# Feature sums of a graph network: four buffers for parts and masks, residues by pairs of visits, a square root's wait moved

## The reference

```python
x = x + _L0(h, edge_attr_16, src, dst, ...)   # 2 rounds: messages, segment_sum over dst, GRU
x = x + _L1(h, edge_index, ...)               # two GCN convolutions, dinv = rsqrt(degree + 1)
x = x + _L2(h, edge_index, edge_attr_16, ...) # mean of neighbours, last edge's features per node
x = x + _L3(h, edge_index, edge_attr_32, ...) # MLP on edges, segment_sum, GRU
```

## Time and profile before

| | us |
|---|---|
| median of 3 runs | 4950.62 (4948.92 to 4953.69) |
| the profiled execution | 4948.67 |
| its span, first to last instruction | 4946.6 |
| stretch of the feature sums, first mask's start to last mask's | 444 |
| from there to the build's first mask | 85 |

### The profile page before, as it was taken

One profiled execution on the slowest core, in us unless ns is written; L12 is line 12 of the kernel. 1 busy time (PEld: TensorE's weight loads), 2 busy tenths in 40 slices (PEclk: granted clock), 3 DMA queues, 4 the chain that ended last, 5 costly groups with the idle time before them and its releaser, 6 DMA issues. The chain is left out here.

```text
span 4946.6 us, 93310 instructions
## 1 busy us (share of the span) xinstructions
PE 3317.7 (67%) x24444; PEld 2513.4 (51%) x24445; DVE 2832.9 (57%) x7446; ACT 886.4 (18%) x1811; POOL 2097.5 (42%) x2644
## 2 busy tenths in 40 slices
PE   2333277777769889899989744555555666666666
PEld 1222123333329889798989633334444444444445
DVE  6555788777765544311323355555566666666775
ACT  1111113566650022200001100000000000000002
POOL 4666700000000021111111277777777777777770
PEclk6555699888889999999999755555555555555558
DMA  3000000111125424354544322223222333333330
GB/s 141 0 0 0 4 14 33 52 58 58 58 92 172 150 71 159 123 174 156 189 153 158 91 64 64 66 67 70 69 69 71 74 72 75 74 76 73 77 77 19
DMA packets 173539, 403.74 MB, mean 82 GB/s; under 512 B 47902, under 2 KB 109481, under 8 KB 172809
## 3 DMA queue, kind: packets, MB, share of 16 engines
q1 hardware_dynamic: 52409, 259.35, 14.7%
q10 hardware_dynamic: 69360, 91.59, 6.6%
q0 software_dynamic: 51680, 51.82, 6.0%
HBM read 359.52 MB, written 43.07 MB: 81 GB/s over the span
## 5 line engine op out<-in xcount | busy, mean ns | idle before, releaser
L697 POOL DMA_INDIRECT scr<-ptable,src_i x1566 | 1522.1, 972 | 481.6 <-issue 398.3
L666 POOL COPY late<-late 128x256 f32<-128x256 f32 (+1 forms) x65 | 25.8, 398 | 1949.6 <-POOLq L664 1949.6
L1030 PE MATMUL ps_front<-scr,arena 128*128 128x192 bf16 x7203 | 612.2, 248 | 67.2 <-PEq L1028 67.2
L1139 PE MATMUL ps_front<-stat_w,scr 128*128 128x392 fp8e4 x2064 | 494.2, 370 | 239.4 <-PEq L1143 214.3
L1030 PEld LDWEIGHTS ps_front<-scr,arena 128*128 128x128 fp8e4 x7203 | 601.0, 98 | 76.9 <-issue 74.9
L900 ACT ACTIVATE arena<-arena 128x384 f32<-128x384 f32 x309 | 161.6, 523 | 1859.9 <-ACTq L899 1859.9
L952 PE MATMUL ps_front<-arena 128*128 (+1 forms) x930 | 176.7, 363 | 434.3 <-PEq L950 434.3
L1651 DVE TENSOR_TENSOR scr<-scr,late 128x384 bf16<-128x384 f16 x1024 | 360.5, 352 | 183.7 <-DVEq L1650 176.4
L1139 PEld LDWEIGHTS ps_front<-stat_w,scr 128*128 128x128 bf16 x2064 | 187.8, 105 | 507.8 <-issue 467.0
L952 PE MATMUL ps_back<-arena 128*128 x924 | 175.5, 363 | 402.0 <-PEq L950 402.0
L1030 PE MATMUL ps_front<-arena 128*128 128x192 bf16 x4802 | 406.4, 248 | 23.1 <-PEq L1028 23.1
(11 more groups left out here) (342 smaller groups left out, 5043.5 us busy)
## 6 DMA issues: line engine op xcount, KB each, us to landing
arena<-a_dram SPq DMA_DIRECT2D x245, 784.0 KB, 4.3
arena<-low_dram ACTq DMA_DIRECT2D x309, 192.0 KB, 3.3
a_dram<-arena SPq DMA_DIRECT2D x49, 784.0 KB, 3.3
arena<-in_e32g ACTq DMA_DIRECT2D x309, 96.0 KB, 3.3
scr<-ptable,src_i POOLq DMA_INDIRECT x1566
arena<-in_e16p SPq DMA_DIRECT2D x1, 13387.5 KB, 35.3
x<-in_x_nm SPq DMA_DIRECT2D x1, 1664.0 KB, 8.2
out_nm<-x SPq DMA_DIRECT2D x1, 1664.0 KB
```

The lines of the kernel that those rows point to most:

```text
L697: pool.indirect_dma_start(grow[:, g % RING, j, :], None, ptable, bass.IndirectOffsetOnAxis(ap=src_i[:, g * GC + j:g * GC + j + 1], axis=0) ...
L1030: last = pe.matmul(ps_z[b % 2][:, 0:3 * H], amat[b][:, i, :], hsp[k % 2][:, i, :], start=(i == 0), stop=(i == NT - 1))
L1139: return pe.matmul(bank_w[i][:, 0:WC], oh_lo[u][:, j, :], oh_hi[u][:, j, :], **{"start": False, "stop": False, **flags})
```

## The change

`eparts` and `otile` move from `stat_w` to `scr`, which is free at that time, and have four buffers each (VR = 4), taken by the visit's number modulo four; ScalarE and TensorE use them accordingly. VectorE issues the mask of visit n ahead of `multiplied()`, where it was behind it. GpSimd works on two visits at a time: first both first subtractions, then both second ones, each with its wait. VectorE's wait for the square root (`s_sqd`) moves from before L1828 to behind the build. The shapes and the number of operations stay as they were.

```diff
         stat_w = sb("stat_w", [P, 2 * NW])
-        eparts = stat_w[:, 0:6 * SC * E16W].rearrange("p (b k j f) -> p b k j f", b=2, k=3, j=SC)
-        otile = stat_w[:, 6 * SC * E16W:6 * SC * E16W + P * SC].bitcast(bf16).rearrange("p (b d j) -> p b d j", b=2, j=SC)
+        VR = 4
+        parts_end = VR * 3 * SC * E16W
+        eparts_w = scr[:, 0:parts_end]
+        eparts = eparts_w.rearrange("p (b k j f) -> p b k j f", b=VR, k=3, j=SC)
+        otile = scr[:, parts_end:parts_end + VR * P * SC // 2].bitcast(bf16).rearrange("p (b d j) -> p b d j", b=VR, j=SC)
...
-            def residues(n, m, c):
-
-                b = m % 2
-                features = e16a[:, ds(c, SC), :]
-                pool.wait_ge(s_e3f, 1)
-                pool.sem_inc(s_e3f, -1)
-                pool.tensor_tensor(eparts[:, b, 1, :, :], features, upper(features), ALU.subtract).then_inc(s_pool, 1)
-                pool.wait_ge(s_pool, 1)
-                pool.sem_inc(s_pool, -1)
-                pool.tensor_tensor(eparts[:, b, 2, :, :], eparts[:, b, 1, :, :], eparts_h[:, b, 1, :, :],
-                                   ALU.subtract).then_inc(s_e3, 1)
-
-            all_visits(pool, 5, 6, residues)
+            def residues(pair):
+
+                for b, c in pair:
+                    features = e16a[:, ds(c, SC), :]
+                    pool.wait_ge(s_e3f, 1)
+                    pool.sem_inc(s_e3f, -1)
+                    pool.tensor_tensor(eparts[:, b, 1, :, :], features, upper(features), ALU.subtract).then_inc(s_pool, 1)
+                for b, c in pair:
+                    pool.wait_ge(s_pool, 1)
+                    pool.sem_inc(s_pool, -1)
+                    pool.tensor_tensor(eparts[:, b, 2, :, :], eparts[:, b, 1, :, :], eparts_h[:, b, 1, :, :],
+                                       ALU.subtract).then_inc(s_e3, 1)
+
+            with pool.Fori(0, NV // 4) as i:
+                four = [(m, c) for m, (c,) in enumerate(visits(pool, i, 5, 6))]
+                residues(four[0:2])
+                residues(four[2:4])
+            residues([(m, c) for m, (c,) in enumerate(visits(pool, NV // 4, 5, 6))][0:NV % 4])
...
                     links = has(-3) + (has(-1) and has(1))
                     if links:
                         linked(links)
+                    v.tensor_tensor(otile[:, m, :, :], drel[:, m, :].unsqueeze(1).broadcast_to([P, P, GC]),
+                                    itiles[:, :, :], ALU.is_equal).then_inc(s_oh, 1)
                     if has(-2):
                         multiplied()
-                    v.tensor_tensor(otile[:, m % 2, :, :], drel[:, m, :].unsqueeze(1).broadcast_to([P, P, GC]),
-                                    itiles[:, :, :], ALU.is_equal).then_inc(s_oh, 1)
-                    if has(-2):
                         summed(before, (m + 2) % 4).then_inc(s_v, 1)
                     if has(2):
                         relative(c2, t2, (m + 2) % 4).then_inc(s_v, 1)
 
-                v.sem_inc(s_e3f, 2)
-                v.sem_inc(s_e1f, 2)
+                v.sem_inc(s_e3f, VR)
+                v.sem_inc(s_e1f, VR)
...
             v.reciprocal(dinv[:, :], dinv[:, :]).then_inc(s_sq, 1)
-            v.wait_ge(s_sqd, 1)
-            v.sem_inc(s_sqd, -1)
             link(v.tensor_scalar(rcnt[:, :], deg[:, :], 1.0, None, ALU.max))
...
             with v.Fori(DENSE, NT) as t:
                 build_tile(t)
+            v.wait_ge(s_sqd, 1)
+            v.sem_inc(s_sqd, -1)
             v.wait_ge(s_lgd, 1)
             v.sem_inc(s_lgd, -1)
```

More of the change, by code:

```diff
@@ L172, in gnn @@
         stat_w = sb("stat_w", [P, 2 * NW])
-        eparts = stat_w[:, 0:6 * SC * E16W].rearrange("p (b k j f) -> p b k j f", b=2, k=3, j=SC)
-        eparts_h = stat_w[:, 0:6 * SC * E16W].bitcast(bf16).rearrange(
-            "p (b k j f w) -> p b k j f w", b=2, k=3, j=SC, w=2)[:, :, :, :, :, 1]
-        otile = stat_w[:, 6 * SC * E16W:6 * SC * E16W + P * SC].bitcast(bf16).rearrange("p (b d j) -> p b d j", b=2, j=SC)
+        VR = 4
+        parts_end = VR * 3 * SC * E16W
+        eparts_w = scr[:, 0:parts_end]
+        eparts = eparts_w.rearrange("p (b k j f) -> p b k j f", b=VR, k=3, j=SC)
+        eparts_h = eparts_w.bitcast(bf16).rearrange("p (b k j f w) -> p b k j f w", b=VR, k=3, j=SC, w=2)[:, :, :, :, :, 1]
+        otile = scr[:, parts_end:parts_end + VR * P * SC // 2].bitcast(bf16).rearrange("p (b d j) -> p b d j", b=VR, j=SC)
         vis_w = sb("vis_w", [1, VW * 6 + GL])
@@ L777, in features @@
                 act.sem_inc(s_e1f, -1)
-                act.copy(eparts[:, m % 2, 0, :, :], e16a[:, ds(c, SC), :]).then_inc(s_e1, 1)
+                act.copy(eparts[:, m, 0, :, :], e16a[:, ds(c, SC), :]).then_inc(s_e1, 1)
             all_visits(act, 5, 6, features)
@@ L1191, in feature_sums @@
                 for j in range(SC):
-                    last = pe.matmul(bank_w[m][:, 0:3 * E16W], otile[:, m % 2, :, j], eparts_h[:, m % 2, :, j, :],
+                    last = pe.matmul(bank_w[m][:, 0:3 * E16W], otile[:, m, :, j], eparts_h[:, m, :, j, :],
                                      start=j == 0, stop=j == SC - 1)
```

## The result

The changed kernel takes 4884.76 us (median of 4 runs, 4881.64 to 4885.26), the kernel before, beside it, 4951.04 us (median of 4): 66.3 us less, ratio 0.9865 (95%: 0.9849 to 0.988). The profiled execution of after took 4881.64 us and spans 4879.8 us, where before's spans 4946.6: 66.8 us less.

| stretch | before, us | after, us | difference |
|---|---|---|---|
| feature sums, first mask to last | 443.96 | 386.92 | -57.04 |
| last mask to the build's first | 85.23 | 76.14 | -9.09 |
| build | 864.56 | 865.90 | +1.34 |
| edge network | 2005.89 | 2005.55 | -0.34 |
| all else | | | -1.7 |

A forecast was written before the change was run, and what follows sets the result against it. VectorE's sequencer was taken to bound the feature sums. Savings of 55 us there and 9 us from the root's wait sum to 64: 4950.6 - 64 = 4887 us, range 4862 to 4925 (forecast case 4870 to 4906, chance 0.62).

The forecast's parts named there:

- The two terms: Forecast savings: 55 us in the feature sums and 9 us from the wait for the square root.
- part 4: Feature sums: VectorE and GpSimd operations delay each other, 0.17 us a block, leaving a block of 5.06 us.
- The bound: Feature sums: VectorE's sequencer sets the pace; three semaphore instructions cost 0.30 us while the engine idles before the mask.
- Part 1: Mask ahead of multiplied() in the feature sums: short interval 0.97 us instead of 1.26, long 1.98; saves 68 us.
- rival 1: Feature sums: the load at the block's end gains as well, 23 us more, 4864 us; chance 0.09.
- the row of 0.14 us: First visits' gap for one wait and a dispatch; taken to say three semaphore instructions just fit under the mask.
- Part 2: Four buffers in the feature sums: they allow the new order and remove waits next in line; no separate saving.
- Part 3: GpSimd's residues by pairs: removes 0.18 us idle between its subtractions; extra cost of uncovered pairs taken as nothing.
- rival 3: Feature sums don't get shorter, pair order or GpSimd's pace being the bound; only root's 9 us, 4941.5 us; chance 0.07.
- the walk: Stepping through one feature-sum block: L1773 waits 0.06 us twice, the mask 0.05 once, 0.17 us in all.
- rival 2: Feature sums: VectorE and GpSimd exclude each other for whole instructions, 0.69 us a block, 4927 us; chance 0.17.
- Part 5: Square root's wait before L1828 moved behind the build: saves 9.1 us, ends 8.6 and 9.2.

The follow-up runs named there:

- e5: The kernel before with one more increment of an unused semaphore per visit, ahead of the mask: 4979.57 us, ratio 1.0053.
- e1: The changed kernel with the mask put back behind multiplied(), four buffers, pairs and moved root's wait kept: 4946.27 us, ratio 0.9984.
- e7: The changed kernel with GpSimd's subtractions cut to one chunk in six, so sums incomplete: 5567.89 us on a slower chip, ratio 0.9867.
- e6: The changed kernel with two more increments of an unused semaphore behind the mask: 5619.35 us on a slower chip, ratio 0.9955.
- e3: The changed kernel with GpSimd working visit by visit and the parts' buffers back at two, masks at four: 5616.81 us on a slower chip, ratio 0.996.
- e2: The changed kernel with GpSimd doing one visit at a time instead of pairs, buffers still four: 4884.58 us, ratio 0.9861.
- e11: The changed kernel with the link's wait moved behind the mask and GpSimd doing one visit at a time: 4880.08 us, ratio 0.9853.
- e10: The changed kernel with the link's wait also moved behind the mask, GpSimd's pairs kept: 4884.31 us, ratio 0.9861.
- e4: The kernel before with only the wait for the square root moved behind the build: 4946.09 us, ratio 0.9985.
- e12: As e11, with buffers handed back two at a time, every other visit, halving the increments: 5587.71 us on a slower chip, ratio 0.988.
- e8: The changed kernel with each block's first mask issued ahead of the load of table values: 5580.01 us on a slower chip, ratio 0.9891.

## Why the prediction was right

It forecast 4887 us, the time is 4884.8; saved were 66.3 us in place of 64. The two terms came as forecast, 57 and 9 us for 55 and 9, and not by errors that cancel, save in part 4.

**The bound.** Right. The prediction read from the first visits that a semaphore instruction costs a tenth; e5 puts 0.093 us on it by adding one. e1 excludes that buffers or pairs were what held the stage.

**Part 1.** Right in both intervals: 0.97 forecast and 0.967 measured where GpSimd stays away (in e7 all three are 0.967 to 0.978), and 1.98 forecast and 1.991 measured across the block's end. That one was 1.990 before, so moving the three instructions brings nothing there, and rival 1 didn't come. The cover for them just fits, as the row of 0.14 us said; e6 shows that 0.04 us are to spare.

**Part 2.** Right that the buffers only allow the order. It didn't price what each ring is worth, though: with the parts' ring at two, 42 us of the changed kernel's stage are lost (e3; 48 against e2). GpSimd's mean load said nothing on this, one delay of 0.4 us in a block did it. The masks' ring at two with the new order wasn't tried, since it would not be correct: the new order writes a mask before it has waited for the products of two visits back, which may still be reading the buffer that it overwrites.

**Part 3.** What uncovered pairs cost was taken as nothing, and in the total it can hardly be seen; in the trace the pairs cost 0.07 us a block, 5 us of stage (e2; e11 against e10: 5.9). What kept rival 3 small was right: in e2 GpSimd has the idle time back that the pairs remove, and isn't the bound.

**Part 4.** Size right, split half right. Forecast: L1780 late by 0.06 us twice a block and the mask by 0.05 once, 0.17, block 5.06. Measured: L1780 late by 0.07 twice, the mask not at all inside the loop (median 558 ns; two of 309 took over 570, one in the first block and one in the last), block 5.035. The step that failed is in the walk: it placed the mask at + 0.97 although it had just made L1780 in front of it 0.06 us late. Carried on, the mask comes at + 1.04, the L625 that was to hold it up ends 0.14 us later (240.86 + 0.355 against 241.07), and less the 0.15 us nothing is left. The forecast so took 0.05 x 77 = 3.9 us too much for the mask and, with 0.07 for 0.06 twice, 1.5 too little for L1780, which makes the 2.4 us by which the 57.0 measured exceed its 54.7 (0.71 x 77). The rule "what is left of the other, less 0.15 us" holds in the new rows, at its far end too: where GpSimd starts with the mask, it takes 0.77 us, so 0.415 longer, and 0.558 less 0.15 is 0.41 (e3, e12).

The Trainium skill, "SBUF — State Buffer", section "Who interferes with whom", says that the second to issue fully blocks until the first finishes. By these rows the later one does wait (but not always where both start within 0.01 us, last section), 0.15 us less than that; and an operation of six elements a partition like L1780 loses 0.07 us and not the 0.27 that were left of L621 (240.90 less 240.63). So rival 2 (4927 us) didn't come.

**Part 5.** Right: 9.09 us in after, 9.04 alone (e4), 9.1 forecast. The idle time at the next wait, the one for TensorE, is 0.26 us with and without the root's (L1834 in before: 0.26 too), so of the 0.5 us allowed for it nothing was needed.

**The rest.** 1.3 us more in the build and 2 less elsewhere are of the size by which these stretches differ between executions (build 864.0 to 867.4, edge network 2001.7 to 2011.2 in the runs on these chips), and nothing is read from them.

## What to carry to other kernels

When idle time ends in an engine's own queue, count the queue's instructions between two long operations, and see how many fit under the one before: here a mask of 0.558 us covers three and a dispatch, and reordering them brought 57 us with no operation made faster. After that the cover is used up: moving the link's wait brought 3 us of the stage, moving the load cost 4. What shortens the interval then is an instruction fewer, and it must not hand a buffer back later. Price a ring of buffers by the worst meeting of the two engines, not by their mean load.

## What the runs showed of the hardware

- A semaphore instruction in VectorE's queue took 0.093 us each time (e5: four intervals, each 0.093 us longer), as much at the block's end as inside it. The one behind a wait started 0.11 us after it.
- Where a GpSimd operation and a mask start within 0.01 us of each other, one of them pays and the other doesn't, and the order of the starts doesn't say which: in e12 the L621 of 238.79 took 0.77 us and the mask of 238.80 0.55; in e8 the mask of 239.94 took 0.76, beside an L625 that began as closely before it and took 0.35.
- The trace's name for a releaser can change with no change of time: the 0.44 us before the mask are put to the queue in before and to PE in e1, with the products in before the idle time began in both.
- The same kernel before took 4951 to 4954 us in three of the comparisons, and 5645 and 5651 us in two, on other chips. The feature sums are alike to 0.002 us an interval; in the traces of the experiments the edge network takes 2670 to 2678 us there instead of 2002 to 2011, the build 881 to 894 instead of 864 to 867. These are the groups of GpSimd's row gathers from 1900 to 4000 us, of after and then of e3 (busy us, mean ns | idle us before, releasers):

```profile
L704 POOL DMA_INDIRECT scr<-ptable,src_i x965 | 936.8, 971 | 298.4 <-issue 245.0 <-POOLq L702 53.3
```

```profile
L699 POOL DMA_INDIRECT scr<-ptable,src_i x720 | 698.0, 969 | 468.5 <-POOLq L697 253.7 <-issue 214.7
```

A gather is issued as fast on either (971 and 969 ns), but on the slow chip GpSimd waits 254 us instead of 53 at L697, for a free buffer of gathered rows: the transfers, or what empties the buffers, are slower there. Which of the two, no run here tells.
